# The last FFN of a decoder layer kept feature-major, its maxima taken without transposes, and its w2 products in runs of 16

## The reference

```python
def act_quant(x):
    scale = 127.0 / jnp.clip(jnp.max(jnp.abs(x), axis=-1, keepdims=True), 1e-05)
    return jnp.clip(jnp.round(x * scale), -128, 127) / scale
...
def _L0_ffn_ref(x, w1, conv_w, conv_b, w2):
...
    h = bit_linear(x, w1)
    h = depthwise_conv1d(h.transpose(0, 2, 1), conv_w, conv_b)
    h = h.transpose(0, 2, 1)
    h = jax.nn.silu(h)
    return bit_linear(h, w2)
x = x + _L0_attn_ref(_layernorm(x, axis=-1), L0_attn_Wqkv, L0_attn_bqkv, L0_attn_Wout, L0_attn_bout)
...
x = x + _L0_ffn_ref(_layernorm(x, axis=-1), L0_ffn_w1, L0_ffn_conv_w, L0_ffn_conv_b, L0_ffn_w2)
```

## Time and profile before

| | |
|---|---|
| median of 3 runs | 3618.28 us |
| profiled execution, time | 3615.1 us |
| its span, first to last instruction | 3613.4 us |
| mean granted clock of PE, share of full | 0.953 |
| PE, DVE, ACT, POOL busy | 3183.6, 2336.2, 1842.0, 1079.9 us |

### The profile page before, as it was taken

The page is one execution under the profiler, slowest core; times in us unless marked ns, Lnnn a source line. Parts: engine busy times, 40 slices in busy tenths (PEclk is TensorE's granted clock), DMA queues, the critical chain, the costliest instruction groups (busy, mean ns, idle before and its releaser), DMA issues. The chain is left out here.

```text
span 3613.4 us, 55879 instructions
## 1 busy us (share of the span) xinstructions
PE 3183.6 (88%) x19218; PEld 2307.8 (64%) x19218; DVE 2336.2 (65%) x4146; ACT 1842.0 (51%) x2979; POOL 1079.9 (30%) x829
## 2 busy tenths in 40 slices
PE   6998999999999999599996998599999998376687
PEld 5776666666666666377774777488878886143244
DVE  5563888888888888445644888444444445567766
ACT  3331888888888888322222222222222221467676
POOL 2343213112211311242322454211111110356555
PEclk9999999999999999799997999799999999688998
DMA  6775113212212221555536343321111101320111
GB/s 212 243 248 164 56 56 90 61 55 80 71 58 64 82 63 56 182 194 187 200 128 199 117 146 102 127 69 31 37 34 41 42 30 41 94 65 18 47 47 42
DMA packets 239599, 350.47 MB, mean 97 GB/s; under 512 B 31792, under 2 KB 129104, under 8 KB 239440
## 3 DMA queue, kind: packets, MB, share of 16 engines
q1 hardware_dynamic: 208784, 291.46, 25.2%
q0 software_dynamic: 8640, 31.77, 2.6%
q10 hardware_dynamic: 22016, 25.17, 2.0%
HBM read 210.68 MB, written 137.64 MB: 96 GB/s over the span
## 5 line engine op out<-in xcount | busy, mean ns | idle before, releaser
L863 DVE CUSTOM_DVE_ANT_0 attend_scores<-attend_scores,attend_bias_table 128x1024 f32<-128x1024 f32 x512 | 630.4, 1231 | 163.4 <-PE attend_scores L717 157.0
L790 ACT ACTIVATE attend_probs<-attend_scores,attend_neg_max 128x1024 f32<-128x1024 f32 x512 | 571.0, 1115 | 136.6 <-DVE attend_neg_max L863 126.7
L729 PE MATMUL attend_turned<-attend_ident,attend_probs 128*128 128x128 f32 x4096 | 556.5, 275 | 11.4 <-DVE attend_probsT L871 11.2
L729 PEld LDWEIGHTS attend_turned<-attend_ident,attend_probs 128*128 128x128 f32 x4096 | 471.9, 140 | 121.1 <-DVE attend_probsT L871 28.1
L717 PE MATMUL attend_scores<-attend_k_stack,attend_q_stack 96*128 96x512 f32 x1024 | 374.4, 447 | 14.4 <-DMA attend_q_stack<-qk_parts 9.7
L798 ACT COPY attend_probsT<-attend_turned 128x512 f32<-128x512 f32 x640 | 359.1, 583 | 24.8 <-PE attend_turned L729 23.1
L2207 DVE TENSOR_TENSOR cross_ffn_h_lo<-cross_ffn_hidden,cross_ffn_h_hi 128x512 fp32r<-128x512 f32 x128 | 96.5, 758 | 362.3 <-ACT cross_ffn_h_hi L2104 361.7
L744 PE MATMUL attend_out_acc<-attend_probsT,attend_v_in 128*32 128x256 f32 x4096 | 312.9, 389 | 0.7 <-DVE attend_out_full L881 0.7
L691 POOL TENSOR_TENSOR attend_out_parts<-attend_out_full,attend_out_parts 128x256 fp32r<-128x256 f32 x64 | 46.5, 726 | 855.5 <-ACT attend_out_parts L805 855.5
L871 DVE COPY attend_probsT<-attend_turned 128x512 f32<-128x512 f32 x384 | 263.3, 686 | 1.0 <-PE attend_turned L729 1.0
L717 PEld LDWEIGHTS attend_scores<-attend_k_stack,attend_q_stack 96*128 96x128 f32 x1024 | 153.9, 189 | 171.8 <-issue 169.2
(11 more groups left out here) (296 smaller groups left out, 6624.3 us busy)
## 6 DMA issues: line engine op xcount, KB each, us to landing
qk_parts<-qkv_qk_out SPq DMA_DIRECT2D x64, 512.0 KB, 3.2
attend_k_stack<-qk_parts SPq DMA_DIRECT2D x192, 128.0 KB, 2.5
attend_q_stack<-qk_parts SPq DMA_DIRECT2D x192, 128.0 KB, 2.7
qkv_wq_raw<-L_ffn_w POOLq DMA_DIRECT2D x16, 1024.0 KB, 7.7
o_parts<-attend_out_parts ACTq DMA_DIRECT2D x64, 256.0 KB, 2.5
mix_in_o_in<-o_parts SPq DMA_DIRECT2D x32, 512.0 KB, 6.7
qkv_x_in<-x SPq DMA_DIRECT2D x8, 1024.0 KB, 6.2
v_rows<-qkv_v_out SPq DMA_DIRECT2D x32, 256.0 KB, 3.4
```

The lines of the kernel that those rows point to most:

```text
L729: last = pe.transpose(turned[:, x, c], probs[:, i % 2, k * P:(k + 1) * P], ident[:, :])
L790: act.activation(probs[:, i % 2], scores[:, i % 2], ACT.Exp, bias=neg_max[:, i % 4:i % 4 + 1], scale=-1.0, accum_out=den[:, qg % 2, j, h:h ...
L863: dve.tensor_tensor_reduce(scores[:, i % 2], scores[:, i % 2], bias_table[:, h, at:at + T], -1.0, BIG, ALU.add, ALU.min, neg_max[:, i % 4: ...
```

## The change

`quantised_ffn` is rewritten; the other stages stay. There are no phases any more. The work is cut into 128 blocks of 128 features by 512 tokens (a `unit` u is half a sequence, 16 blocks), and all engines walk through the same list of slots s. In slot s each engine does its step for the block that lies a fixed number of slots behind:

- PE: the block's 4 products (L2391) for block s. Behind them in every fourth slot 16 products by w2 for one token tile (L2417), then, once per unit, the transposes of the column maxima (`turn_max`) and the product that spreads the token scales over all partitions (`spread_scale`), and once per sequence 128 products with a single column (`edge_products`, L2382), which give the two tokens at the seam between the halves, one from each side.
- ACT: `set_edge` (a one-column copy into `y`), the centre and right taps of block s, silu of block s-2, and once per unit the copy of the spread scales to `scale_row`. DVE has no centre taps any more.
- POOL: `add_right` for block s (L2355), then `scale_block` for block s-22 (L2361), `h * scale_row`.
- DVE: `dequantise` of block s (L2504), `add_left` of block s-1 (L2512), `round_block` of block s-23 (L2551), which writes `hqT` in bf16 straight in the layout that w2 products need; then, for every fourth block, the maximum over four blocks per token and partition (L2521), once per unit the maximum of those four (L2526) and, two slots on, the scales (L2532 to L2543); and in every fourth slot `finish` of a token tile (L2558).

So `h` is never transposed. SP issues the tokens and factors of sequence 1 ahead of w2T, and PE makes the first sequence's seam products before it waits for w2T.

```diff
+    TURN_AT, SPREAD_AT, ROUND_AT = HB + 3, HB + 5, HB + 6
+    PRODUCT_AT = ROUND_AT + HB + 1
+    END = (UNITS - 1) * HB + PRODUCT_AT + HB + 2
@@ sync
                 load_x(0)
                 sp.dma_start(w1T[:, :, :], w1T_parts.rearrange("k p n -> p k n")).then_inc(w_loaded[0], 16)
+                load_x(1)
                 sp.dma_start(w2T[:, :, :], w2T_parts.rearrange("f p n -> p f n")).then_inc(w_loaded[1], 16)
@@ gpsimd
-                        pool.tensor_tensor(hq[:, t % 2, g * D:(g + 1) * D], h_rounded[:, g], round_down[:, :].to_broadcast([P, D]),
+                def add_right(i):
+                    pool.wait_ge(right_ready, i + 1)
+                    pool.wait_ge(left_added, i + 1)
+                    pool.tensor_tensor(conv[:, i % CR], conv[:, i % CR], right_tap[:, i % 2], ALU.add).then_inc(right_added, 1)
+                def scale_block(i):
+                    u, f = divmod(i, HB)
+                    pool.wait_ge(scale_row_ready, u + 1)
+                    past(pool, hq_ready, i - 1)
+                    pool.tensor_tensor(h_scaled[:, i % 2], h[:, u % 2, f], scale_row[:, u % 2], ALU.mult).then_inc(h_scaled_ready, 1)
+                for s in range(END):
+                    if s < SLOTS:
+                        add_right(s)
+                    i = block_at(s, ROUND_AT)
+                    if i is not None:
+                        scale_block(i)
@@ tensor
-                        last = pe.transpose(big[:, g, k * P:(k + 1) * P], h[:, g * 4 + k, t * P:(t + 1) * P], ident[:, :])
-                        last = pe.transpose(turned[:, s, k * P:(k + 1) * P], hq[:, t % 2, at:at + P], ident16[:, :])
+                    j, part = product_at(s)
+                    if part == 3:
+                        for p in range(4):
+                            w2_product(j, p)
@@ vector
+                def dequantise(i):
+                    past(dve, centre_ready, i - 1)
+                    past(dve, right_ready, i - 1)
+                    past(dve, left_added, i - 1)
+                    dve.wait_ge(h_ready, i + 1)
...
+                    dve.tensor_tensor(y[:, s, i % 2, 1:HALF + 1], acc[:, i % ACC], unit_row[:, b % 2, s * HALF:(s + 1) * HALF], ALU.mult)\
+                        .then_inc(y_ready, 1)
+                def find_max(i):
+                    if f % 4 == 3:
+                        dve.wait_ge(silu_done, i + 1)
+                        dve.tensor_reduce(group_max[:, f // 4], h[:, u % 2, f - 3:f + 1].rearrange("p f t -> p t f"), AX.X, ALU.max,
+                                          apply_absolute_value=True).then_inc(maxed, 1)
+                    if f == HB - 1:
+                        dve.wait_ge(maxed, (u + 1) * 4)
+                        dve.tensor_reduce(col_max[:, :], group_max[:, :, :].rearrange("p g t -> p t g"), AX.X, ALU.max).then_inc(col_max_ready, 1)
+                def round_block(i):
+                    dve.wait_ge(h_scaled_ready, i + 1)
+                    if f == 0:
+                        past(dve, out_ready, (u - 1) * HT)
+                    dve.tensor_scalar(hqT[:, u % 2, f], h_scaled[:, i % 2], ROUND, -ROUND, ALU.add, ALU.add).then_inc(hq_ready, 1)
+                for s in range(END):
+                    if s < SLOTS:
+                        dequantise(s)
+                    i = block_at(s, 1)
+                    if i is not None:
+                        add_left(i)
+                    i = block_at(s, ROUND_AT + 1)
+                    if i is not None:
+                        round_block(i)
+                    i = block_at(s, 3)
+                    if i is not None:
+                        find_max(i)
```

More of the change, by code:

```diff
@@ L2443, in _, with silu @@
                 act.wait_ge(const_step, 6)
[L2445 to L2446 removed]
+                def silu(i):
+                    u, f = divmod(i, HB)
                     act.wait_ge(right_added, i + 1)
[L2448 to L2457 removed]
@@ new lines, in _ @@
+                for s in range(END):
+                    if s < SLOTS:
+                        set_edge(s)
+                        taps_of(s)
+                    i = block_at(s, 2)
+                    if i is not None:
+                        silu(i)
+                    u = half_at(s, SPREAD_AT)
+                    if u is not None:
+                        act.wait_ge(spread_ready, u + 1)
+                        past(act, h_scaled_ready, (u - 1) * HB)
+                        act.copy(scale_row[:, u % 2], spread[:, :]).then_inc(scale_row_ready, 1)
```

415 lines of the change are left out of this document (190 added, 225 removed).

## The result

Compared within the same runs, the kernel before took 3618.14 us (3616.22 to 3622.75, 4 runs) and the changed one 3865.55 us (3864.57 to 3865.89, 4 runs): the ratio is 1.0681, interval 1.0663 to 1.0700. The forecast was 3817, its range 3780 to 3885. The profiled execution had a span of 3863.0 us, 249.6 more than before; 198.6 were forecast.

A forecast was written before the change was run, and what follows sets the result against it. DVE and POOL were taken to wait for each other in every heavy slot. Start 4.5 + 3.6, light slots 57.1, heavy 569.8, tail 60.5 make 695.5 us against 496.9: 3618.3 + 198.6 gives 3817 us, range 3780 to 3885.

The forecast's parts named there:

- heavy slot: Slots with scaling and rounding: DVE waits for both POOL operations, no overlap, 4.44 us each; 106 slots plus extras 569.8 us.
- the strided maxima: Rival, 23 in 100: maxima reading with a 2 KB step are slow; half a lost read per element +43, 3860 us.
- maxima over 2.4 us: Sign of being wrong: a maximum over four blocks on DVE lasting longer than 2.4 us.
- POOL busy about 60% of the stage: Sign of being right: POOL's busy share over the last stage, about 60%.
- w2T term: Stage start: 1.5 MB of second-sequence loads ahead of w2T delay block products by 4.5 us, bounds 0 and 15.7.
- filling: Stage start, until the first left tap: first dequantisation and a centre tap, 3.6 us.
- Light slots: First 22 left taps, no scaling or rounding: 2.19 us each, 57.1 us with maxima and scales.
- Tail: Stage end: 22 remaining roundings at 1.68 us, last maxima and scales, then four tiles of w2 products: 60.5 us.
- M and C: DVE's maximum over four blocks, 2.24 us less 0.08, and last maximum per half, 2.36; priced from reductions over neighbours.
- PE gets in the way: Rival, 5 in 100: three bursts of one-column edge products at 1.2 GHz delay DVE, +24, 3841 us.
- The engines overlap after all: Rival, 6 in 100: scaled blocks are always ready for rounding, heavy slots average 3.97 us, 3694 us.
- Faster than before: Rival, 4 in 100: overlap, and POOL and DVE run side by side; heavy slot 2.40 us, 3527 us.

The follow-up runs named there:

- best kernel: Four blocks of a column stored side by side, against the kernel with later rounding, centre tap in PSUM and w2T loaded first: 3656.14 us, ratio 1.0099.

## Why the prediction was right

The direction, the mechanism and most of the size were right. The heavy slot was forecast from DVE's and POOL's order alone at 4.44 us and came at 4.37; the wait ahead of each rounding at about 2.7 and came at 2.67; the left tap of the heavy slots is unstretched, as forecast. The later rounding shows that this is the cause and not a picture of it: moving one wait gives back 169 us.

The size was partly luck of a wide range. The measured 3865.55 lies outside the forecast's own range of 3795 to 3840. The stated range up to 3885 holds it only because two thirds of a rival, the strided maxima, had been let into it. Of the signs that the prediction named for being wrong, one came (maxima over 2.4 us) and a second in part (DVE waited for PE after the start, 4.4 us in two waits, both in the light slots). Its "POOL busy about 60% of the stage" does not fit its own sum (106 x 2.50 in 569.8 us is 47%); measured were 44%.

The miss is 51.0 us of span (3863.0 against 3812), by the prediction's own steps:

- Ahead of the stage, 4.8 us: VectorE's last operation of the unchanged stages ended at 3087.73 and not 3082.92. In the traces of the twelve kernels of the experiments, with the same stages ahead, it ended between 3085.2 and 3091.6. The profiled execution of before was also 3.2 us below the median of its runs. So most of these 4.8 us is how quick that one execution was; whether one or two of them belong to the change stays open.
- The start's w2T term was 4.5 and is 4.4 (first product 9.17 us later, less 4.8); the filling was 3.6 and is 4.2.
- Light slots: 57.1 forecast, 67.3 measured. Six strided maxima (the sum had five here and one too many in the heavy slots) give +8.2 for the step and +1.35 for the one not counted. Two waits for PE, 1.85 and 2.58 us, were put at nothing: PE stood behind the transposes of the maxima, then behind the spread product. The rest is -3.8: slots without a maximum, scales or such a wait took 1.90 on average and not 2.19. The forecast added the left tap's full 0.74 to POOL's 1.27, but a tap that waits for POOL ends 0.55 after POOL lets go (1.08 of 1.28 in the earlier trace rows).
- Heavy slots: 569.8 forecast, 602.1 measured (597.7 from the left tap at 3197.19 to the one at 3794.92, and a last slot of 4.4). 32 strided maxima give +43.8, the one counted too many -2.2, 0.07 less per slot -7.4, and -1.9 is spread over the rest. The kernel with maxima over neighbours has its heavy slots 42.2 us shorter, its light ones 8.4.
- Tail: 60.5 forecast, 63.7 measured; with maxima over neighbours it is 1.6 shorter.

So **the mis-sized term is M and C**: 2.24 us was taken from reductions over neighbours, and with the step it is 3.61, or 1.76 ns for each of the 2048 elements (over neighbours 2.28 us, 1.11 ns). 40 of them at +1.37 make 55 us, and leaving the step out gave 55.0. The other errors nearly cancel: without the 4.8 us ahead of the stage they come to -8.6. The forecast with that term right would have been 3872. The value was chosen with the argument that every one-input row has it. That is not so (the rounding's 512 elements take 0.427 us), and no such row had a step, so the rows could not speak on it. "Vector Engine (DVE) Microarchitecture Reference" in the Trainium skill, section on the SBUF access granule, had 1.73 ns a column for a source that hops on every element, and by that the sum was 3869; the trace agrees at 1.76. The 1.76 has the operation's fixed cost in it; less the 0.17 us that the rows of 1024 and 512 elements leave as fixed, it is 1.68. The page's example of a one-source operation at full rate does not carry over to this reduction.

Of the rivals, *strided maxima are slow* was true, on top of the forecast mechanism and not instead of it. *PE gets in the way* was refuted for the edge bursts. The first ran at a granted clock of 0.50, the lower of the two levels, and took 3.55 us (28 ns a product), where at most 7.2 us were allowed and 14 feared at that clock. The three others ran at 1.00 and took 3.37. The windows of the first and the third (busy us of PE, PEld, DVE, ACT and POOL; the clock is the third number from the end):

```profile
3115.10:3118.70 3.60, 3.55 (x128) 3.48 (x128) 0.00 (x0) 0.00 (x0) 0.00 (x0) 0.50 1.07 369
3373.90:3377.40 3.50, 3.50 (x131) 3.32 (x129) 3.50 (x2) 0.00 (x0) 0.00 (x0) 1.00 0.02 5
```

DVE waited for block products four times, for 8.5, 1.01, 1.85 and 2.58 us, and each time before the first heavy slot. *The engines overlap after all* is what the later rounding makes of the kernel; its working gave 3694 with 2.24 us a maximum, and the measured 3696.68 has the strided ones in it, so the overlapped slots are cheaper than that rival had them: four take 14.78 us with a strided maximum, where it had 15.9 with one over neighbours. *Faster than before* needs DVE and POOL to run side by side, and the stretched operations above speak against it.

Four things make up the 247 us, as far as the edits show it: 169 the serial slot, 55 the maxima's step (25 where the step moves to silu and the scaling, 3681.13 to 3656.14), about 4 the load of sequence 1, and a rest of some 20 that no run traced to a cause. The parts were not all measured on the same base and need not add up. Why the best kernel is still 36 us behind the one before is not shown. Its rows have a candidate: 66 roundings that each take 0.57 us more than their work are 38 us in 250. But freeing the left tap of 0.32 us a slot gave back only 15.6 us, w2T's 4 among them, where 34 were hoped for, so such a sum says where time sits and not what its removal would give. No edit that took the rounding's stretching away without a new wait was found.

## What to carry to other kernels

When one engine's step releases two steps of another and the first engine needs the second of these in the same slot, the slot is the sum of both engines. Write down who releases whom before adding the engines' busy times; here one more slot of lag was worth 169 us and the shorter maxima 55. When a dense access is traded for a strided one, price it with a strided row, or take the slow bound as the value, and count the operations on the other side that get the step.

## What the runs showed of the hardware

- DVE's left tap (two inputs in SBUF, 512 columns) takes 0.74 us alone and, in the kernel with the later rounding, up to 1.77 beside POOL; with one of its inputs in PSUM its mean is 0.74 in every kernel. The f32 rounding with one input, 0.43 alone, is stretched to 1.47 as well. Even an operation of four columns is: in the fastest kernel one of those that make the scales takes 1.35 us in six of the eight half sequences, where the changed kernel has 0.20. "SBUF — State Buffer" in the Trainium skill, section on the two separate sides, describes an exclusive lock on a shared port pair that holds for a whole instruction, taken by DVE operations with two SBUF inputs or in a two-port mode; these rows agree: the stretched left tap above starts while POOL runs and ends 0.56 us after POOL. That the rounding runs in a two-port mode is not shown by a run; 512 columns in 0.43 us, against 0.74 for the left tap, fit it.
- Who gets in first can matter by itself: 17 us for moving PE's run and a 0.74 us finish by one slot with both inputs of the left tap in SBUF, and nothing with one of them in PSUM and the products in quarters.
- A step of 16 bytes costs the other engines too. ACT's silu over 512 columns went from 614 to 1120 ns when it wrote with that step. POOL's scaling, where nothing stretches it, went from 1.26 us (the changed kernel) to 1.52 (the rounding ahead of the left tap) when it read with that step.
- 128 bf16 products with a single column, each with its own weights, took 3.55 us at a granted clock of 0.50 and 3.37 at 1.00: the clock hardly matters to them.
